# Five loads of x and four stores of a table, each issued as 120 and 8 partitions

## The chip, the core and the metric

The kernel runs on one core of a Trainium2 chip. Its time is the device time of one execution in microseconds; where several runs are named, the median of them. The core has five engines: TensorE (PE in the rows; PEld is its weight load), VectorE (DVE), ScalarE (ACT), GpSimd (POOL) and SyncE (SP). Transfers are issued from SP, ACT or POOL and carried out by 16 DMA engines that all queues share. SBUF, the on-chip memory, has 128 partitions.

## The reference

One layer of graph attention over N = 8192 nodes with F = 128 features, behind a layer norm. The adjacency matrix has some four ones in a row of 8192.

```python
h = jnp.maximum(_layernorm(x, axis=-1), 0.0)
# _L0_gnn_ref(h, adj, W, a):
h = x @ W
s_src, s_dst = h @ a[:F_out, 0], h @ a[F_out:, 0]
e = leaky_relu(s_src[:, None] + s_dst[None, :], negative_slope=0.2)
e = jnp.where(adj > 0, e, -9e15)
h_prime = softmax(e, axis=1) @ h
# result
x = x + h_prime
```

x is 8192 x 128 float32 (4 MB), adj is 8192 x 8192 int32 (256 MB), and the output has the shape of x.

## The kernel before

**Work.** The kernel never forms the dense attention. It reads all of adj once, finds in each row where the ones stand, and gathers only the rows of those neighbours from a table in DRAM. The table has one row of 130 numbers for each node: the 128 features of h @ W and the two scores of the node.

**First stage, the table.** SP issues five loads of x (L266, groups of 8, 8, 16, 16 and 16 tiles of 128 nodes). For each group VectorE computes the mean and variance of every row and from them 1/sqrt by Newton steps (`statistics`, L556 on); it waits for the load by the semaphore `x_loaded[k]`. ScalarE and GpSimd normalize (L431, L342), TensorE transposes (L1007), ScalarE takes the ReLU (L441), TensorE multiplies with W (L1017), ScalarE copies the rows of the table out of PSUM (L446). When a quarter of the rows is there, ScalarE issues its store to DRAM (`store_rows`, L458, four stores of 1040 KB: after steps 5, 9 and 13 of 16, and one at the end). GpSimd waits for the four semaphores `rows_stored[k]` before its first gather, since a gather may touch any row.

**Second stage, the batches.** adj comes in 32 batches of 256 rows. A batch is 8 units of 128 x 2048 numbers, and one load brings two units (L271, 2048 KB, 128 loads in all). `adj_buf` holds 8 units, so four loads are in flight or in use. SP issues the first four loads behind those of x, without a wait. Each later load waits until the two units of the batch before, whose place it takes, have been turned into masks (`mask_ready`). ScalarE makes the masks (L467, one instruction for a unit), apart from four of batch 0 that VectorE makes (L589). TensorE packs the masks into words (L1046, L1048), VectorE finds the set bits, GpSimd issues 14 gathers for each batch (L361), and VectorE forms the weighted sums into `x_all` (L820), from which SP stores the output at the end.

**Order.** Every engine runs its own list in program order, and semaphores tie them together. A transfer counts 16 on its semaphore when all of it has landed. A transfer issued from SP or ACT is queued behind the earlier ones of that issuer; the two issuers' queues are served side by side.

Of the kernel before, what the change touches and what calls it, by code (L numbers as in the profile page):

```python
# [4 lines left out]
P = 128  # L5
# [3 lines left out]
QUARTER = TILES // 4  # L9

STAT_GROUPS = [(0, 8), (8, 16), (16, 32), (32, 48), (48, 64)]
FOUR = 4
# [22 lines left out]
PART = N // PARTS  # L35
PART_BITS = BITS // PARTS
STORE_RUNS = ((0, 5), (5, 10), (10, 14), (14, 15))
SLOTS = 8
OWN = 6
SHARED = SLOTS - OWN  # L40
COLUMNS = 2 * OWN + SHARED
WIDE = 16
ROW = F + 2
S_COL, D_COL = F, F + 1
MORE = WIDE - SLOTS
REC = MORE + 4
# [36 lines left out]
def gat_kernel(nc, x, adj, W, a, out):  # L83
# [5 lines left out]
    mean_place, node_rows = table[0:1, :], table[1:1 + N, :]  # L89

    ctx = ExitStack()
    with ctx:
        def sb(name, shape, dt):
            return ctx.enter_context(nc.sbuf_tensor(name, shape, dt))

        def sem(name):
            return ctx.enter_context(nc.semaphore(name))
# [3 lines left out]
        mask_buf = sb("mask_buf", [P, UNITS, PART], bf16)  # L101
        gathered = sb("gathered", [P, BUFS, BATCH * SLOTS * ROW], f32)
        g_cols = [gathered[:, buf, :].rearrange("p (k n) -> p k n", n=ROW) for buf in range(BUFS)]

        g_view = [[g_cols[buf][:, b * OWN:b * OWN + SLOTS, :] for b in range(BATCH)] for buf in range(BUFS)]

        rows_all = gathered[:, :, :].rearrange("p a (t n) -> p (a t) n", n=ROW)

        x_all = sb("x_all", [P, TILES, F], f32)
# [43 lines left out]
        top = sb("top", [P, BATCH, WIDE], f32)  # L153
        skip = sb("skip", [P, BATCH, SLOTS], f32)
        index = sb("index", [P, BUFS, BATCH * SLOTS], u32)
        mine = sb("mine", [P, BATCH, SHARED], f32)
# [53 lines left out]
        x_loaded = [sem(f"x_loaded{k}") for k in range(len(STAT_GROUPS))]  # L210
# [5 lines left out]
        rows_stored = [sem(f"rows_stored{k}") for k in range(4)]  # L216
# [23 lines left out]
        def rows_of(dram, t, tiles):  # L240

            q, c = t // FOUR, t % FOUR
            return dram[q * FOUR * P:(q + 1) * FOUR * P, :].rearrange("(p c) n -> p c n", c=FOUR)[:, c:c + tiles, :]
# [5 lines left out]
        def group_of(i):  # L249

            return sum(1 for end in GROUP_ENDS if i > end)

        stores_in = [16 * (sum(1 for lo, _ in STORE_RUNS if group_of(lo * FOUR // BATCH) == g)
                           + (1 + BATCH if end == LAST else 0)) for g, end in enumerate(GROUP_ENDS)]
# [8 lines left out]
        @block.sync  # L263
        def _(sp):
            for k, (lo, hi) in enumerate(STAT_GROUPS):
                sp.dma_start(x_all[:, lo:hi, :].rearrange("p (q c) f -> p q (c f)", c=FOUR), x[lo * P:hi * P, :].rearrange("(q p c) f -> p q (c f)", p=P, c=FOUR)  # L266
                             ).then_inc(x_loaded[k], 16)

            def load_two(i, u):
                source = rows_of(adj, i * BATCH + u // PARTS, 1)[:, 0, u % PARTS * PART:(u % PARTS + 2) * PART]  # L270
                sp.dma_start(adj_buf[:, u:u + 2, :].rearrange("p u n -> p (u n)"), source).then_inc(adj_loaded[u // 2], 16)  # L271

            def load_batch(i):
                for u in range(0, UNITS, 2):

                    sp.wait_ge(mask_ready, (i - 1) * UNITS + u + 2)
                    load_two(i, u)

            def store_fours(lo, hi, group):

                sp.wait_ge(out_ready, hi * FOUR // BATCH)
                sp.dma_start(out[lo * FOUR * P:hi * FOUR * P, :].rearrange("(q p c) f -> p q (c f)", p=P, c=FOUR),
                             x_all[:, lo * FOUR:hi * FOUR, :].rearrange("p (q c) f -> p q (c f)", c=FOUR)
                             ).then_inc(out_stored[group], 16)

            def store_tiles(t, tiles, ready, group):
                sp.wait_ge(out_ready, ready)
                sp.dma_start(rows_of(out, t, tiles), x_all[:, t:t + tiles, :]).then_inc(out_stored[group], 16)

            for u in range(0, UNITS, 2):  # L290
                load_two(0, u)
            for i in range(1, BATCHES):
                load_batch(i)
            for lo, hi in STORE_RUNS:
                store_fours(lo, hi, group_of(lo * FOUR // BATCH))
            store_tiles((LAST - 1) * BATCH, BATCH, LAST, group_of(LAST))
            for b in range(BATCH):
                store_tiles(LAST * BATCH + b, 1, BATCHES + b, group_of(LAST))

            for g in range(GROUPS):  # L300
                sp.wait_ge(out_stored[g], stores_in[g])
            sp.wait_ge(w_stored, 16 * GROUPS)

            sp.wait_ge(verdict, 1)
            unfit_nodes = sp.value_load(unfit_n[0:1, 0:1], min_val=0, max_val=N)
            with sp.If(unfit_nodes > 0):

                sp.nop().then_inc(dn_out, 16)
                with sp.Fori(0, TILES) as t:

                    sp.wait_ge(dn_o, t + 1)
                    sp.dma_start(dense_adj, adj[bass.ts(t, P), :]).then_inc(dn_adj, 16)
                    sp.dma_start(x_row, x[bass.ts(t, P), :]).then_inc(dn_x, 16)
                    sp.dma_start(sd_row, node_rows[bass.ts(t, P), S_COL:ROW]).then_inc(dn_x, 16)
                    with sp.Fori(0, TILES // 4) as j:

                        sp.wait_ge(dn_mm, t * (TILES // 4) + j + 1)
                        sp.dma_start(h_blk, node_rows[bass.ts(j, 4 * P), 0:F].rearrange("(b p) f -> p b f", p=P)).then_inc(dn_h, 16)
                    sp.wait_ge(dn_o, t + 2)
                    sp.dma_start(out[bass.ts(t, P), :], o_row).then_inc(dn_out, 16)  # L320
                sp.wait_ge(dn_out, 16 * (TILES + 1))
# [3 lines left out]
        def _(pool):  # L325
# [26 lines left out]
            pool.wait_ge(mean_taken, 1)  # L352
            nc.gpsimd.dma_start(mean_place, mean_row[0:1, :]).then_inc(mean_stored, 16)
            for k in range(4):
                pool.wait_ge(rows_stored[k], 16)
            pool.wait_ge(mean_stored, 16)
            pool.wait_ge(sd_ready, 1)

# [54 lines left out]
        def _(act):  # L413
# [41 lines left out]

            def store_rows(k):
                act.wait_ge(rows_ready, (k + 1) * (FOURS // 4))
                act.dma_start(node_rows[k * QUARTER * P:(k + 1) * QUARTER * P, :].rearrange("(q p c) n -> p q (c n)", p=P, c=FOUR),  # L458
                              rows_all[:, k * QUARTER:(k + 1) * QUARTER, :].rearrange("p (q c) n -> p q (c n)", c=FOUR)
                              ).then_inc(rows_stored[k], 16)  # L460

            def mask(i, u):
                act.wait_ge(adj_loaded[u // 2], 16 * (i + 1))
# [64 lines left out]
        def _(dve):  # L528
# [24 lines left out]

            def statistics(k):
                lo, hi = STAT_GROUPS[k]
                dve.wait_ge(x_loaded[k], 16)  # L556
                settled()
                for t in range(lo, hi):
                    ins = v.bn_stats(stats[:, t - lo], x_all[:, t, :])  # L559
                done.add(ins)  # L560
                settled()
                for t in range(lo, hi):
                    ins = v.bn_aggr(mv_all[:, t, :], stats[:, t - lo])  # L563
                done.add(ins)
                settled()
                done.add(v.tensor_scalar(var_e[:, lo:hi], mv_all[:, lo:hi, 1], EPS, None, ALU.add))
                settled()

                square, factor = newton[:, 0, 0:hi - lo], newton[:, 1, 0:hi - lo]
                done.add(v.tensor_scalar(square.bitcast(i32), var_e[:, lo:hi].bitcast(i32), 1, None, ALU.arith_shift_right))  # L570
                settled()
                done.add(v.tensor_scalar(rstd[:, lo:hi].bitcast(i32), square.bitcast(i32), -1.0, float(MAGIC),
                                         ALU.mult, ALU.add))
                for _ in range(NEWTON_STEPS):
                    settled()
                    done.add(v.tensor_tensor(square, rstd[:, lo:hi], rstd[:, lo:hi], ALU.mult))  # L576
                    settled()
                    done.add(v.scalar_tensor_tensor(factor, square, -0.5, var_e[:, lo:hi], ALU.mult, ALU.mult))  # L578
                    settled()
                    done.add(v.scalar_tensor_tensor(rstd[:, lo:hi], factor, 1.5, rstd[:, lo:hi], ALU.add, ALU.mult))  # L580
                settled()
                v.scalar_tensor_tensor(nbias[:, lo:hi], mv_all[:, lo:hi, 0], -1.0, rstd[:, lo:hi], ALU.mult, ALU.mult  # L582
                                       ).then_inc(rstd_ready, (hi - lo) // FOUR)
# [588 lines left out]
```

## Time and profile before

| what | us |
|---|---|
| median of 3 runs (805.66 to 805.8) | 805.73 |
| the profiled execution: its own time | 804.8 |
| its span, from the first to the last instruction | 803.0 |
| busy: VectorE 606.7, ScalarE 526.8, TensorE 515.2, GpSimd 512.5 | |

The profiled execution is one run; what lies between its span and its own time (1.8 us) is outside the instructions. All starts in the rows below count from the start of the span. The busy times are sums over the whole span, so none of them alone says what bounds a stage.

### The profile page before, as it was taken

The numbers are of one execution on the slowest core, as the hardware profiler recorded it, in microseconds if no ns is written. First come the engines' busy times: TensorE is split into PE (matmuls) and PEld (weight loads), VectorE is DVE, ScalarE is ACT, GpSimd is POOL, SyncE is SP. The second block draws the span as 40 slices with busy tenths as digits, with TensorE's granted clock in tenths as the row PEclk, the third lists the DMA queues.
The fourth block names the chain that finished last, engine by engine and source line by source line (L and its number), as shares of the span: only waits on it lengthen the run. The fifth ranks groups of instructions, "written<-read, shape, count | busy, mean of one in ns | idle before, by whom it ended". The sixth has DMA issues, their size and how long they took to land.

```text
span 803.0 us, 9015 instructions
## 1 busy us (share of the span) xinstructions
PE 515.2 (64%) x1855; PEld 229.5 (29%) x1855; DVE 606.7 (76%) x3167; ACT 526.8 (66%) x371; POOL 512.5 (64%) x522
## 2 busy tenths in 40 slices
PE   3778666766577576666667676676767676656521
PEld 3652222322222232322222222222222232222221
DVE  7956678667776768777779778777786798888984
ACT  3879667676767767766767767676666767676300
POOL 4753776656666665577767666656777756775671
PEclk9888656676855766777666767667666556676655
DMA  8999999999999999999999999999999999999310
GB/s 334 423 386 390 406 403 406 409 411 407 408 408 409 409 407 401 406 398 393 380 406 397 405 396 399 392 408 397 400 389 398 389 399 399 389 380 402 120 37 15
DMA packets 40903, 299.31 MB, mean 373 GB/s; under 512 B 11052, under 2 KB 14034, under 8 KB 24464
## 3 DMA queue, kind: packets, MB, share of 16 engines
q1 hardware_dynamic: 22976, 276.83, 85.3%
q0 software_dynamic: 15328, 17.58, 6.9%
q10 hardware_dynamic: 2544, 4.33, 1.6%
q8 instruction: 15, 0.25, 0.1%
q14 instruction: 40, 0.33, 0.1%
HBM read 304.31 MB, written 8.65 MB: 390 GB/s over the span
## 4 chain that ended last, share of the span: by engine, by line
DMA 68%; DVE 10%; ACT 10%; issue 8%; PE 3%; POOLq 0%; ACTq 0%; DVEq 0%
DMA adj_buf<-in_adj 67%; ACT mask_buf L467 9%; DVE x_all L820 3%; PE banks L1048 2%; DVE stats L559 2%; PE banks L1017 1%; DVE mv_all L563 1%; DMA x_all<-in_x 1%; PE banks L1007 0%; DVE newton L576 0%; DVE rstd L580 0%; DVE newton L578 0%; PE banks L1089 0%; DVE mask_buf L589 0%; ACT work L431 0%
## 5 line engine op out<-in xcount | busy, mean ns | idle before, releaser
L467 ACT ACTIVATE mask_buf<-adj_buf,minus_half 128x2048 bf16<-128x2048 int32 x252 | 493.0, 1994 | 205.9 <-DMA adj_buf<-in_adj 205.4
L361 POOL DMA_INDIRECT gathered<-table,index x448 | 448.5, 1001 | 242.5 <-issue 145.9
L1048 PE MATMUL banks<-mask_buf,bit_ident 128*128 128x512 bf16 x1024 | 388.5, 527 | 99.8 <-ACT mask_buf L467 99.0
L1048 PEld LDWEIGHTS banks<-mask_buf,bit_ident 128*128 128x128 bf16 x1024 | 107.9, 124 | 325.7 <-ACT mask_buf L467 187.7
L820 DVE SCALAR_TENSOR_TENSOR x_all<-gathered,weight,x_all 128x128 f32<-128x128 f32 x512 | 157.7, 348 | 7.2
L635 DVE MAX8 words<-banks 128x8 f32<-128x512 f32 x64 | 44.7, 698 | 119.9 <-PE banks L1048 119.8
L1046 PE MATMUL banks<-key_rows,ones_b 3*128 3x512 bf16 x64 | 31.7, 495 | 119.2 <-ACT mask_buf L467 118.8
L1089 PE MATMUL banks<-x_all,one_hot 128*128 128x128 f32 x128 | 44.0, 445 | 18.3 <-DVE x_all L820 18.3
L1046 PEld LDWEIGHTS banks<-key_rows,ones_b 3*128 3x128 bf16 x64 | 6.1, 95 | 147.8 <-ACT mask_buf L467 145.9
L639 DVE MAX8 words<-rest 128x8 f32<-128x512 f32 x64 | 44.5, 695 | 2.2
L1089 PEld LDWEIGHTS banks<-x_all,one_hot 128*128 128x128 f32 x128 | 36.1, 317 | 27.5 <-DVE x_all L820 19.5
L637 DVE MATCH_REPLACE8 rest<-words,banks 128x512 f32<-128x512 f32 x64 | 43.5, 680 | 0.0
L342 POOL TENSOR_SCALAR work<-x_all,mv_all,rstd 128x128 f32<-128x128 f32 x32 | 30.9, 981 | 17.8 <-DVE nbias L582 15.9
L1090 PEld LDWEIGHTS banks<-max_sum,one_hot 128*128 128x128 f32 x128 | 33.6, 321 | 0.0
L387 POOL DMA_INDIRECT w_gathered<-table,w_index x24 | 24.0, 999 | 8.2 <-issue 6.7
L1090 PE MATMUL banks<-max_sum,one_hot 128*128 128x2 f32 x128 | 26.4, 276 | 0.0
L1074 PEld LDWEIGHTS banks<-rec,one_hot 128*128 128x128 f32 x128 | 22.7, 226 | 10.0 <-DVE one_hot L767 4.5
L784 DVE TENSOR_SCALAR e<-gathered,sd_all 128x8 f32<-128x8 f32 x64 | 13.3, 255 | 14.8 <-DMA gathered<-table,index 13.9
L1074 PE MATMUL banks<-rec,one_hot 128*128 128x12 f32 x128 | 19.8, 266 | 4.3 <-DVE one_hot L767 4.3
L1007 PE MATMUL banks<-ident,work 128*128 128x128 f32 x64 | 13.0, 338 | 14.1 <-ACT work L431 5.8
L1017 PE MATMUL banks<-w_ext,work 128*128 128x130 f32 x128 | 21.9, 326 | 0.0
L1017 PEld LDWEIGHTS banks<-w_ext,work 128*128 128x128 f32 x128 | 19.8, 235 | 1.2 <-ACT work L441 0.9
(162 smaller groups left out, 537.9 us busy)
## 6 DMA issues: line engine op xcount, KB each, us to landing
adj_buf<-in_adj SPq DMA_DIRECT2D x128, 2048.0 KB, 18.7
gathered<-table,index POOLq DMA_INDIRECT x448, 6.4
table<-gathered ACTq DMA_DIRECT2D x4, 1040.0 KB, 14.7
x_all<-in_x SPq DMA_DIRECT2D x3, 1024.0 KB, 10.8
out<-x_all SPq DMA_DIRECT2D x2, 1280.0 KB, 23.0
x_all<-in_x SPq DMA_DIRECT2D x2, 512.0 KB, 5.3
out<-x_all SPq DMA_DIRECT2D x1, 1024.0 KB, 25.5
w_gathered<-table,w_index POOLq DMA_INDIRECT x24, 5.3
```

Source lines behind the costliest of these rows:

```text
L361: nc.gpsimd.indirect_dma_start(g_cols[buf][:, k, :], None, table, bass.IndirectOffsetOnAxis(index[:, buf, k:k + 1], 0), bounds_check=N, oo ...
L467: nc.scalar.activation(mask_buf[:, u], adj_buf[:, u], ACT.Sign, bias=minus_half[:]).then_inc(mask_ready, 1)
L635: done.add(v.max(words[:, b, 0:8], bank))
L637: v.match_replace(rest[:, b], words[:, b, 0:8], bank, -float(1 << BITS)).then_inc(words_read, 1)
L639: done.add(v.max(words[:, b, 8:16], rest[:, b]))
L820: ins = v.scalar_tensor_tensor(at[b], g_view[par][b][:, k, 0:F], weight[:, b, k:k + 1], at[b], ALU.mult, ALU.add)
L1017: ins = mm(banks[:, 2 + 2 * par + b // 2, at:at + ROW], relu_t[par][:, b], w_ext[:], start=True, stop=True)
L1046: mm(bank, ones_b[0:3, :], key_rows[0:3, :], start=True, stop=False)
L1048: ins = mm(bank, bit_ident[:, h * PART_BITS + c], mask_buf[:, u, c * BIT_COLS:(c + 1) * BIT_COLS], start=False, stop=(h == PARTS - 1 and c ...
L1074: ins = mm(banks[:, 3, 0:REC], one_hot[:, i % BUFS, b], rec[:, i % BUFS, b], start=False, stop=False)
L1089: mm(banks[:, bank, 0:F], one_hot[:, i % BUFS, b], x_all[:, i * BATCH + b, :], start=False, stop=False)
L1090: ins = mm(banks[:, bank, F:SUMS], one_hot[:, i % BUFS, b], max_sum[:, i % BUFS, b], start=False, stop=False)
```

## The change

Each of the five loads of x and each of the four stores of the table is issued as two transfers: one for partitions 0 to 119 (`LIGHT = 120`) and, right behind it on the same queue, one for partitions 120 to 127. Both count 16 on the same semaphore, and those who wait for it now wait for 32. The bytes, their places in DRAM and SBUF and all else stay as they were. The loads of adj and the stores of the output are not touched.

```diff
+LIGHT = 120
...
             for k, (lo, hi) in enumerate(STAT_GROUPS):
-                sp.dma_start(x_all[:, lo:hi, :].rearrange("p (q c) f -> p q (c f)", c=FOUR), x[lo * P:hi * P, :].rearrange("(q p c) f -> p q (c f)", p=P, c=FOUR)
-                             ).then_inc(x_loaded[k], 16)
+                place = x_all[:, lo:hi, :].rearrange("p (q c) f -> p q (c f)", c=FOUR)
+                rows = x[lo * P:hi * P, :].rearrange("(q p c) f -> p q (c f)", p=P, c=FOUR)
+                sp.dma_start(place[0:LIGHT], rows[0:LIGHT]).then_inc(x_loaded[k], 16)
+                sp.dma_start(place[LIGHT:], rows[LIGHT:]).then_inc(x_loaded[k], 16)
...
             for k in range(4):
-                pool.wait_ge(rows_stored[k], 16)
+                pool.wait_ge(rows_stored[k], 32)
...
-                act.dma_start(node_rows[k * QUARTER * P:(k + 1) * QUARTER * P, :].rearrange("(q p c) n -> p q (c n)", p=P, c=FOUR),
-                              rows_all[:, k * QUARTER:(k + 1) * QUARTER, :].rearrange("p (q c) n -> p q (c n)", c=FOUR)
-                              ).then_inc(rows_stored[k], 16)
+                place = node_rows[k * QUARTER * P:(k + 1) * QUARTER * P, :].rearrange("(q p c) n -> p q (c n)", p=P, c=FOUR)
+                rows = rows_all[:, k * QUARTER:(k + 1) * QUARTER, :].rearrange("p (q c) n -> p q (c n)", c=FOUR)
+                act.dma_start(place[0:LIGHT], rows[0:LIGHT]).then_inc(rows_stored[k], 16)
+                act.dma_start(place[LIGHT:], rows[LIGHT:]).then_inc(rows_stored[k], 16)
...
-                dve.wait_ge(x_loaded[k], 16)
+                dve.wait_ge(x_loaded[k], 32)
```

SP's list at the start of the program, before; a row is a line, an operation, what it writes and reads, its shape, and how often it stands in a row:

```order
1 L266 DMA x_all<-in_x 128x2x512 x2
2 L266 DMA x_all<-in_x 128x4x512 x3
3 L271 DMA adj_buf<-in_adj 128x4096 x4
4 L271 DMA adj_buf<-in_adj 128x4096 [waits mask_ready] x124
5 L282 DMA out<-x_all 128x5x512 [waits out_ready] x2
```

The same place in the changed kernel:

```order
1 L269 DMA x_all<-in_x 120x2x512
2 L270 DMA x_all<-in_x 8x2x512
3 L269 DMA x_all<-in_x 120x2x512
4 L270 DMA x_all<-in_x 8x2x512
5 L269 DMA x_all<-in_x 120x4x512
6 L270 DMA x_all<-in_x 8x4x512
7 L269 DMA x_all<-in_x 120x4x512
8 L270 DMA x_all<-in_x 8x4x512
9 L269 DMA x_all<-in_x 120x4x512
10 L270 DMA x_all<-in_x 8x4x512
11 L274 DMA adj_buf<-in_adj 128x4096 x4
12 L274 DMA adj_buf<-in_adj 128x4096 [waits mask_ready] x124
```

Ten transfers now stand ahead of the first load of adj, in place of five.

ScalarE's list where the first stage ends, before (the last two copies of table rows, the fourth store, the masks of units 6 and 7 of batch 0, and the first masks of batch 1):

```order
73 L446 COPY gathered<-banks 128x520 [waits projected] x2
74 L458 DMA table<-gathered 128x4x520 [waits rows_ready]
75 L467 ACTIVATE mask_buf<-adj_buf,minus_half 128x2048 [waits adj_loaded3,mask_ready]
76 L467 ACTIVATE mask_buf<-adj_buf,minus_half 128x2048 [waits adj_loaded3]
77 L467 ACTIVATE mask_buf<-adj_buf,minus_half 128x2048 [waits part_packed,adj_loaded0] x2
```

The same place in the changed kernel:

```order
76 L449 COPY gathered<-banks 128x520 [waits projected] x2
77 L463 DMA table<-gathered 120x4x520 [waits rows_ready]
78 L464 DMA table<-gathered 8x4x520
79 L471 ACTIVATE mask_buf<-adj_buf,minus_half 128x2048 [waits adj_loaded3,mask_ready]
80 L471 ACTIVATE mask_buf<-adj_buf,minus_half 128x2048 [waits adj_loaded3]
81 L471 ACTIVATE mask_buf<-adj_buf,minus_half 128x2048 [waits part_packed,adj_loaded0] x2
```

One more issue stands between the last copy and the first mask of this stretch; the three earlier stores have gained one each in the same way.

## Rows read from the trace of the kernel before

**Rows 1.** The page: span and DMA issues (KB each, median us to landing)
```profile
span 803.0 us, 9015 instructions
...
adj_buf<-in_adj SPq DMA_DIRECT2D x128, 2048.0 KB, 18.7
gathered<-table,index POOLq DMA_INDIRECT x448, 6.4
table<-gathered ACTq DMA_DIRECT2D x4, 1040.0 KB, 14.7
```

**Rows 2.** Busy time by stretch, all engines (last three: PE clock, DMA share, GB/s)
```profile
2.00:17.00 15.00, 4.91 (x19) 3.95 (x19) 11.50 (x71) 5.61 (x14) 5.38 (x8) 1.00 0.97 357
17.00:60.00 43.00, 32.73 (x196) 26.75 (x196) 32.51 (x161) 33.98 (x74) 27.33 (x29) 0.84 1.01 407
60.00:80.00 20.00, 15.99 (x61) 5.84 (x61) 12.65 (x62) 19.65 (x12) 6.92 (x7) 0.83 0.99 389
80.00:740.00 660.00, 441.97 (x1505) 180.72 (x1502) 502.31 (x2626) 458.01 (x265) 438.38 (x439) 0.68 1.00 400
```

**Rows 3.** Waits: in total us, times, longest; ACT
```profile
ACT mask_buf L467 <- DMA adj_buf<-in_adj: 205.4, 119, 3.0
```

**Rows 4.** Waits of the DMA queue of SyncE
```profile
SPq L271 <- ACT mask_buf L467: 664.3, 122, 21.5
```

**Rows 5.** Line 271 (loads of adj) from 100 to 700 us
```profile
L271 SPq DMA_DIRECT2D adj_buf<-in_adj x106: 327/328/328, 101.6 to 695.3; - x106
...
DMA to landing us min/median/max: 17.5/18.7/19.7
```

**Rows 6.** Chain that ended last, 0 to 10 us (start, us, what)
```profile
0.75 4.26 DMA x_all<-in_x
...
5.04 1.66 DVE stats L559 x8
```

**Rows 7.** The same chain, 60 to 80 us
```profile
62.10 0.86 ACT mask_buf L467
...
63.99 5.14 ACT mask_buf L467 x3
...
75.46 16.38 DMA adj_buf<-in_adj
```

**Rows 8.** Line 266 (loads of x), whole execution
```profile
L266 SPq DMA_DIRECT2D x_all<-in_x x5: 449/474/699, 0.8 to 3.0; - x5
...
DMA to landing us min/median/max: 4.3/8.6/13.7
```

**Rows 9.** ScalarE in order of time, 50 to 58 us
```profile
55.30 0.59 ACT L446 COPY gathered<-banks 128x520 f32<-128x520 f32 x1 [0.48 <-PE banks L1017]
55.92 0.38 ACTq L458 DMA_DIRECT2D table<-gathered  x1
56.40 2.00 ACT L467 ACTIVATE mask_buf<-adj_buf,minus_half 128x2048 bf16<-128x2048 int32 x1 [0.51 <-ACT gathered L446]
```

**Rows 10.** ScalarE in order of time, 56 to 90 us
```profile
56.40 22.82 ACT L467 ACTIVATE mask_buf<-adj_buf,minus_half 128x2048 bf16<-128x2048 int32 x12 [0.51 <-ACT gathered L446]
79.57 3.90 ACT L467 ACTIVATE mask_buf<-adj_buf,minus_half 128x2048 bf16<-128x2048 int32 x2 [0.35 <-DMA adj_buf<-in_adj]
86.21 3.89 ACT L467 ACTIVATE mask_buf<-adj_buf,minus_half 128x2048 bf16<-128x2048 int32 x2 [2.74 <-DMA adj_buf<-in_adj]
```

**Rows 11.** Line 458, the fourth store alone
```profile
L458 ACTq DMA_DIRECT2D table<-gathered x1: 378/378/378, 55.9 to 55.9; - x1
...
DMA to landing us min/median/max: 8.3/8.3/8.3
```

**Rows 12.** Line 271, the eighth load of adj alone
```profile
L271 SPq DMA_DIRECT2D adj_buf<-in_adj x1: 327/327/327, 60.3 to 60.3; - x1
```

**Rows 13.** GpSimd in order of time: the first gather
```profile
71.25 1.08 POOL L361 DMA_INDIRECT gathered<-table,index  x1 [14.27 <-issue]
```

**Rows 14.** DMA issues of a short store near the end
```profile
out<-x_all SPq DMA_DIRECT2D x1, 256.0 KB, 2.3
```

## The prediction

> **What bounds the kernel now.** I began with the page and the busy time by stretch. The adjacency loads are 128 of 2048 KB [rows 1], 268 MB against some 17 MB for x, table and output. From 80 to 740 us the DMA engines are busy all the time (share 1.00, 400 GB/s) while the busiest computing engine, VectorE, works 502 of 660 us [rows 2]. The waits say the same: ScalarE waited 119 times, 205.4 us in all, for a load of adj before a mask [rows 3], and SP waited 664.3 us for masks before it could issue the next load [rows 4]. So there is a loop: load, mask, next load into the same place. From the first to the last of 106 loads pass 593.7 us, so 593.7 / 105 = 5.65 us for each; a load lands 18.7 us after its issue [rows 5], which is 3.3 loads. Something always stands in the queue, the transfers run back to back, and the end is set by how soon the DMA engines are through with all of adj. After the last load comes a tail of computation that simply moves with it.
>
> The first stage is different. Its chain goes through the first load of x (4.26 us), then VectorE's statistics [rows 6], then ScalarE and TensorE. From 56.40 to 79.2 ScalarE makes twelve masks without a pause; the next mask waits 0.35 us for its load, the one after 2.74 us [rows 10]. So at 79 us ScalarE and the DMA engines are level, and from there the DMA engines lead.
>
> **The change, part by part.** It removes no byte. It adds nine issues, and it may change how the bytes fall on the 16 engines. I number three terms.
>
> *Term 1, five more issues on SP.* One issue of a load of x takes 0.449 to 0.699 us, median 0.474 [rows 8]. Only the first group is urgent: VectorE starts at 5.04, right when the load has landed at 0.75 + 4.26 = 5.01 [rows 6]. The second piece is issued 0.45 to 0.5 us behind the first, and the wait is now for both. If all of that shows, the first stage starts 0.5 us later; if the small piece lands beside the large one, 0. I take 0.4, near the issue's own time, since the small piece can't be requested before. The later four loads have cover: their issues end at 3.6 us now and at some 6 us then, and VectorE is still at work on earlier groups. The first loads of adj go out 5 x 0.5 = 2.5 us later, but they stand behind x in the queue: the last load of x, issued at 3.0, needs 13.7 us [rows 8], up to 16.7. What covers them is that backlog; without it they would cost 2.5 us.
>
> *Term 2, four more issues on ACT.* One takes 0.378 us [rows 11]. The first three lie in a stretch in which ScalarE's issue runs beside its computing, and I give them nothing (all three on the path would be 1.1 us). The fourth does not: the last copy runs until 55.89, the store is issued at 55.92 for 0.38, and the first mask starts at 56.40 after 0.51 us of idle time [rows 9]. Behind that mask wait all the others, the eighth load of adj, which SP issues at 60.3 when units 6 and 7 are masked [rows 12], and the masks at 62.1 to 75 that are on the chain [rows 7]. So +0.38, taken as 0.4. GpSimd now waits for all eight pieces of the table. The last store landed at 55.9 + 8.3 = 64.2 [rows 11] and the first gather started at 71.25 [rows 13], so 7 us of cover lie there, and a store later by 1 or 2 us costs nothing.
>
> *Term 3, which engines carry the bytes.* 128 partitions over 16 engines are 8 each, and 120 are 8 each for 15. If the large piece goes to 15 engines, one engine is left without any of x and of the table, and the 8 small rows fall on others. No row shows the engines apart. What rows say is that all transfers of 128 partitions give each engine the same, so the load of adj as a whole lands when the slowest engine is through. If the spared engine is that one, it has a head start into the stream. How large? Not the whole of what it is spared: before 60.3 us SP holds back the loads, and an engine without work just idles. The head start counts from the eighth load on, issued at 60.3 [rows 12]. A lone store of 256 KB lands 2.3 us after its issue [rows 14], of which 0.6 us is moving it at 407 GB/s [rows 2]; the rest, 1.7 us, is what passes before and after the data. So the eighth load could begin to flow at 60.3 + 1.7 = 62.0, while the fourth store is not through until 64.2. The spared engine gains up to 2.2 us. Upper bound: the whole of one store's share, 1040 KB (1.065 MB) / 407 GB/s = 2.6 us. Lower bound: 0, if the spared engine is not the last. I take 2.2. From then on this engine has always something queued (3.3 loads), so the head start is kept up to the last load. The sum for the likeliest case is 0.4 + 0.4 - 2.2 = -1.4 us. That both delays count in full in that case is because the spared engine now waits for the issue of the eighth load, which they move.
>
> The Trainium skill's page "DMA: Bandwidth & Descriptors", section "Why a DMA increments its semaphore by 16 and not by 1", says that a transfer uses the largest number of engines up to 16 that divides its outer dimension, the lowest-numbered ones; and its section "Latency and other measured facts" calls engines 7 and 15 usually the slower ones. By these two the large piece spares engine 15 and the small one goes to engines 0 to 7. No row here shows it. Against the change speaks the same page's section "Rules for kernel authors": two transfers to disjoint partition halves share the same engines, so use one. By that alone the sum would be terms 1 and 2, +0.8 us.
>
> The sum is made against the profiled execution (span 803.0 us [rows 1], its own time 804.8, 0.9 us below the median 805.73): span 801.6. On the median: 805.73 - 1.4 = 804.3.
>
> **The rivals.**
>
> *A, the spared engine is the slowest one:* 804.3, as above; by its bounds (terms 1 and 2 together 0 to 1.9, term 3 between 0 and 2.6) from 803.1 to 807.6, most of it from 803.2 to 805.5. Chance 0.45. For it speaks that the share of the engines is 1.00 and yet the rate falls from 407 to 400 GB/s [rows 2], as it would if one engine lagged behind; but the gathers' small transfers explain that as well.
>
> *B, the slowest engine gets the small pieces.* The end is later. Its price: x is 4.19 MB and the table 4.26 MB, together 8.45 MB / 407 GB/s = 20.8 us of moving for an even spread; an engine that carries nine rows in place of eight needs 1/8 more, 2.6 us. It counts in full if that engine has never been idle since 2 us, and rows 2 give shares of 0.97, 1.01 and 0.99 up to 80 us. Terms 1 and 2 fall away here, since the backlog covers them. 805.73 + 2.6 = 808.3. It decides from the point at which the slowest engine is among those that carry the extra rows; nothing later heals it, as that engine stays the last. Were it not the last, ScalarE would see 0.5 to 2.5 us more of waiting at 79 us and nothing at the end. Chance 0.14. By the Trainium skill's page named above, this is the case in which engine 7 and not engine 15 is the slowest.
>
> *C, nothing binds.* The slowest engine is among those with 8 rows as before, or the bytes are spread over 16 engines in another way. Terms 1 and 2 shift only work that the backlog covers: 805.7, up to 806.5 if the shift reaches the stream. Chance 0.24. Waits at 79 and 86 us would hardly change.
>
> *D, a larger head start.* The spared engine is the last one already before 60 us, and the third store's share (2.6 us) lies ahead of its eighth load too. 804.3 - 2.6 = 801.7. Against it: the fourth store was through 3.9 us after the eighth load was issued, little more than one store's share and the latency. Chance 0.13.
>
> *E, the small pieces are slow in themselves.* Ten more issues delay VectorE's first group by the length of a whole first load, 4.26 us [rows 6], instead of 0.4. The first stage moves by that, so does ScalarE's run of masks, which is level with the DMA engines at 79 us: 805.73 + 3.9 - 2.2 = 807.4 with the head start. Chance 0.04.
>
> **How the numbers follow.** What a measurement of this kernel can tell from no change is about 0.2%, 1.6 us. Case A gives faster beyond that (below 804.1) in a good four tenths of its chance, 0.20, else no difference, 0.25; D gives faster, 0.13; C gives the same, 0.22, and slower 0.02; B slower, 0.12, and same 0.02; E slower or same, 0.02 and 0.02. Sums: faster 0.33, same 0.51, slower 0.16. The range leaves out the lower half of D (0.06) and the upper half of B with the tail of E (0.08): 801.8 to 808.2.
>
> **What the profile of the changed kernel would show.** Term 1: VectorE's first statistics at 5.4 instead of 5.04. Term 2: two issues of about 0.38 us behind the last copy, the first mask at 57.2 instead of 56.40, and the eighth load at 61.1 instead of 60.3. Term 3: the loads from the eighth to about the twelfth land no sooner, since 15 engines have the same work as before, but ScalarE waits less in the stretch behind, and the last issue of adj is some 1.4 us earlier; the time for a load from 100 us on is unchanged at 5.65 us when taken late in the stream. Wrong would be: a last load later than before (B), or one shifted by exactly the first stage's delay (then the backlog covers nothing). The prediction falls if the stream's own pace changes, since nothing that I count touches it.

## The result and the profile after

The changed kernel takes 816.04 us (median of 4 runs, 815.29 to 817.54), the kernel before in the same session 805.69 us (4 runs, 805.33 to 805.8): 10.35 us more, a ratio of 1.0132 (95% interval 1.0114 to 1.0149). Forecast were 804.3 us, in a range from 801.8 to 808.2. It is slower, and by four times what the dearest of the rivals gave.

The page of the changed kernel: its span and the DMA queues (packets, MB, share of the 16 engines).

```profile
span 814.4 us, 8992 instructions
...
q1 hardware_dynamic: 23011, 276.83, 85.4%
```

The span is 11.4 us longer than in [rows 1]; the queue's bytes and its share are the same as before to a tenth. So no byte was added, and the longer span holds as much more time in packets. The busy time by stretch says where (last two columns: DMA share, GB/s):

```profile
2.00:17.00 15.00, 4.82 (x19) 3.95 (x19) 10.75 (x67) 4.86 (x12) 4.63 (x7) 1.00 0.98 209
17.00:60.00 43.00, 26.88 (x162) 23.69 (x163) 31.33 (x160) 29.30 (x71) 28.07 (x28) 0.76 1.02 376
60.00:80.00 20.00, 15.47 (x77) 6.84 (x77) 12.62 (x62) 16.43 (x13) 1.02 (x2) 1.00 0.97 361
80.00:740.00 660.00, 438.59 (x1467) 177.83 (x1495) 493.64 (x2577) 459.61 (x265) 441.67 (x442) 0.66 1.01 401
```

In [rows 2] the first stretch moved 357 GB/s, here it moves 209 at the same share of 0.98: the engines are as busy and carry little more than half. Missing are 148 GB/s over 15 us, 2.22 MB; 31 GB/s over the 43 us to 60, 1.33 MB (the last loads of x fall into it); and 28 over the 20 us to 80, 0.56 MB. That is 4.11 MB, 10.3 us at the 400 GB/s of the stream: the whole loss, and over half of it is made before 17 us. From 80 us on nothing has changed, 401 GB/s against 400. The loads of adj from 100 to 700 us (line 274 is line 271 of before):

```profile
L274 SPq DMA_DIRECT2D adj_buf<-in_adj x107: 327/328/328, 100.6 to 699.2; - x107
...
DMA to landing us min/median/max: 17.5/18.7/19.6
```

(699.2 - 100.6) / 106 = 5.65 us for a load, landing after 18.7, as in [rows 5]. The stream has its old pace and starts later. The chain that ended last, in the first 40 us:

```profile
4.86 2.88 SPq L270
7.78 23.30 DMA adj_buf<-in_adj
31.53 1.48 issue
```

Before, the chain went through VectorE's statistics [rows 6]; now it goes through the first load of adj, which stands behind x in the queue and lands at 7.78 + 23.30 = 31.1 us. In the first stage VectorE waited once for x before, 1.5 us; now that wait is 2.3 us, and a new one of 5.6 us for adj has joined it. The waits of VectorE from 0 to 60 us (total, times, longest):

```profile
DVE mask_buf L593 <- DMA adj_buf<-in_adj: 5.6, 1, 5.6
DVE stats L563 <- DMA x_all<-in_x: 2.3, 1, 2.3
```

And ScalarE in order of time where the first stage ends:

```profile
61.96 0.59 ACT L449 COPY gathered<-banks 128x520 f32<-128x520 f32 x1 [0.47 <-PE banks L1021]
62.58 0.34 ACTq L463 DMA_DIRECT2D table<-gathered  x1
62.95 2.41 ACTq L464 DMA_DIRECT2D table<-gathered  x1
65.46 2.00 ACT L471 ACTIVATE mask_buf<-adj_buf,minus_half 128x2048 bf16<-128x2048 int32 x1 [2.91 <-issue]
```

The last copy starts 6.66 us later than in [rows 9], and the second of the two issues takes 2.41 us, where one took 0.38; the first mask of this stretch starts at 65.46 instead of 56.40.

The profile has no row for when a load of x in two pieces has landed as a whole. The trace records each engine's own increment of the semaphore, and the last of them is the landing. Worked out from these records, landing of the five loads in us from the start of each kernel's span, for all kernels of this study that touch x or the stores; the row of the changed kernel is the second (the expectations quoted below name some of them up to 0.1 us off):

```
before          5.0    7.5   10.4   13.1   16.8
after           5.8    8.7   14.5   20.6   26.4
x_only          5.9    8.9   14.7   21.0   26.9
x_columns       5.6    7.2   10.2   12.9   15.6
x_64_64         6.0    8.4   13.2   18.0   23.3
x_112_16        5.2    8.6   13.0   17.7   22.3
x_last          5.0    7.5   10.2   13.7   20.0
stores_only     5.0    7.5   10.4   13.1   16.2
```

The fifth load lands 9.7 us later than before, which is nearly the whole loss of 10.35. The same records show 25 increments for each of the changed loads: one at the issue and 15 landings for the piece of 120 partitions, one at the issue and 8 for the piece of 8. So the large piece does run on 15 engines, as term 3 supposed. What it supposed beside that, that each of the 15 takes as long as before, is false.

### The profile page after: what moved, and what is told of

Same layout as the page of the kernel before. It is cut to its first block, busy times and chain, and to the rows that moved or that the text cites. A ratio compares the mean times of both kernels' runs of the same rounds, so it can differ in the third digit from the quotient of the medians.

```text
span 814.4 us, 8992 instructions
## 1 busy us (share of the span) xinstructions
PE 512.3 (63%) x1823; PEld 228.4 (28%) x1855; DVE 604.7 (74%) x3167; ACT 526.9 (65%) x371; POOL 513.4 (63%) x522
## 4 chain that ended last, share of the span: by engine, by line
DMA 71%; ACT 11%; issue 9%; DVE 6%; PE 2%; SPq 1%; ACTq 0%; POOLq 0%; DVEq 0%
DMA adj_buf<-in_adj 71%; ACT mask_buf L471 8%; DVE x_all L824 2%; ACT work L434 1%; PE banks L1052 1%; ACT prob L485 1%; PE banks L1021 1%; SPq L270 1%; ACT gathered L449 0%; PE banks L1011 0%; ACT work L444 0%; SPq L269 0%; DVE rest L641 0%; PE banks L1093 0%; DVE words L643 0%
## 5 line engine op out<-in xcount | busy, mean ns | idle before, releaser
L1093 PE MATMUL banks<-x_all,one_hot 128*128 128x128 f32 x128 | 41.8, 426 | 18.8 <-DVE x_all L824 18.8
L1093 PEld LDWEIGHTS banks<-x_all,one_hot 128*128 128x128 f32 x128 | 33.8, 298 | 26.6 <-DVE x_all L824 19.9
L1094 PEld LDWEIGHTS banks<-max_sum,one_hot 128*128 128x128 f32 x128 | 31.9, 306 | 0.0
## 6 DMA issues: line engine op xcount, KB each, us to landing
adj_buf<-in_adj SPq DMA_DIRECT2D x128, 2048.0 KB, 18.7
```

The lines of the kernel that those rows point to most:

```text
L1093: mm(banks[:, bank, 0:F], one_hot[:, i % BUFS, b], x_all[:, i * BATCH + b, :], start=False, stop=False)
L1094: ins = mm(banks[:, bank, F:SUMS], one_hot[:, i % BUFS, b], max_sum[:, i % BUFS, b], start=False, stop=False)
```

## The experiments

### Which half of the change costs

Of the kernel before, only the loads or only the stores were cut:

```diff
 # x_only
+                sp.dma_start(place[0:120], rows[0:120]).then_inc(x_loaded[k], 16)
+                sp.dma_start(place[120:128], rows[120:128]).then_inc(x_loaded[k], 16)
```

> Only the five loads of x are issued as 120 and 8 partitions; the stores stay whole. Theory P (the loads themselves run slowly: in the changed kernel the fifth load of x had landed at 26.5 us in place of 16.8, and all transfers behind it are that much later): the loss is nearly all here, 9 to 10 us over before, 815 us. Rival Q (the stores: ScalarE's last issue took 2.41 us, and GpSimd's first gather waited for the pieces): under 1 us over before, 806 us. Rival R (the number of issues as such): 5 of 9 issues, about half of the loss, 811 us.

Measured: 815.76 us against 805.22 (ratio 1.0126, 1.0101 to 1.0152), 10.5 us over.

```diff
 # stores_only: each store as [0:120] and [120:128]
-                pool.wait_ge(rows_stored[k], 16)
+                pool.wait_ge(rows_stored[k], 32)
```

> Only the four stores of the table are issued as 120 and 8 partitions; the loads of x stay whole. Theory P: no loss, 805 to 806 us; if the engine that is spared by a piece of 120 partitions is the slowest of the 16, a gain of up to 2.2 us less 0.4, so 804 us. Rival Q: nearly all of the loss, 812 us or more. Rival R: 4 of 9 issues, 810 us. The last issue on ScalarE takes 0.3 to 0.4 us by P, since the queue isn't late, and 2.4 us by Q.

Measured: 806.08 us (1.0017, 1.0002 to 1.0031), 0.9 us over. So the loads of x carry the whole loss (theory P), and rival Q falls: the stores do not cost it. Rival R, the number of issues as such, does not fit either (it had 811 and 810 us). ScalarE in the kernel with the cut stores:

```profile
55.84 0.59 ACT L446 COPY gathered<-banks 128x520 f32<-128x520 f32 x1 [0.47 <-PE banks L1020]
56.46 0.34 ACTq L458 DMA_DIRECT2D table<-gathered  x1
56.83 1.20 ACTq L461 DMA_DIRECT2D table<-gathered  x1
58.13 2.00 ACT L470 ACTIVATE mask_buf<-adj_buf,minus_half 128x2048 bf16<-128x2048 int32 x1 [1.70 <-issue]
```

Even with the loads of x whole, the last issue took 1.20 us where P expected 0.3 to 0.4, and the first mask started 1.73 us later than in [rows 9]. No head start appeared. The store packets themselves are not slower: their median (2080 B each) is 89 ns in the kernel before and 89 ns with the cut stores.

### Is it the number of pieces?

```diff
 # x_columns: 128 partitions in both pieces, half of each partition's bytes
+                half = (hi - lo) // FOUR // 2
+                sp.dma_start(place[:, 0:half], rows[:, 0:half]).then_inc(x_loaded[k], 16)
+                sp.dma_start(place[:, half:], rows[:, half:]).then_inc(x_loaded[k], 16)
```

> The five loads of x are issued as two pieces each, both over 128 partitions, each with half of the bytes of a partition; as many issues as in the changed kernel. Theory P (what costs is how the partitions are cut): the fifth load lands at 17 to 17.5 us, time 805.7 to 806.3 us. Rival R (the number of issues): 811 us or more, as in the run with x alone.

Measured: 805.77 us (1.0003, 0.9987 to 1.0019), no difference, with ten issues as in the change. The fifth load landed at 15.6 us, sooner even than before. Ten transfers in place of five cost nothing; what costs is where the partitions are cut.

### Fifteen engines, or ports?

```diff
 # x_64_64
+                sp.dma_start(place[0:64], rows[0:64]).then_inc(x_loaded[k], 16)
+                sp.dma_start(place[64:128], rows[64:128]).then_inc(x_loaded[k], 16)
```

> The five loads of x are issued as two pieces of 64 partitions. Two forms of theory P: by P1 (the pieces collide at the side of SBUF: at any time the engines write to partitions that reach only half of the ports), the loads of x take twice as long here too, the fifth lands at 26 to 27 us, and the time is 815 us. By P2 (a transfer on 15 engines, or an uneven one, is slow), 64 partitions are 4 for each of 16 engines, nothing is slow, and the time is 806 us.

Measured: 812.64 us (1.0086, 1.0062 to 1.011), 7.4 us over, the fifth load at 23.3 us. All 16 engines take part here (32 landings for each load), and it is slow. P2 is refuted, for it had 806. P1 had the direction, but 815 and 26 to 27 us were too much. The busy time from 6 to 12 us, when SP's queue moves nothing but x, shows it best: first with whole columns, then with 64 and 64 partitions.

```profile
6.00:12.00 6.00, 0.56 (x2) 0.50 (x2) 5.45 (x36) 1.45 (x5) 1.22 (x2) 1.00 1.02 385
```

```profile
6.00:12.00 6.00, 0.56 (x2) 0.50 (x2) 5.45 (x35) 1.13 (x4) 0.90 (x2) 1.00 1.07 220
```

385 against 220 GB/s at full share: 0.57. The changed kernel has 216 in the same stretch:

```profile
6.00:12.00 6.00, 0.56 (x2) 0.50 (x2) 5.45 (x36) 1.32 (x4) 1.09 (x2) 1.00 1.03 216
```

```diff
 # x_112_16
+                sp.dma_start(place[0:112], rows[0:112]).then_inc(x_loaded[k], 16)
+                sp.dma_start(place[112:128], rows[112:128]).then_inc(x_loaded[k], 16)
```

> The five loads of x are issued as 112 and 16 partitions, so each piece can be spread over all 16 engines, 7 and 1 partitions for each. The fifth load lands between the two known cases (16.8 us whole, 26.8 us with 120), at 20 to 23 us, and the time is 808 to 812 us. Theory P2 (only a transfer on fewer than 16 engines is slow): 806 us.

Measured: 810.25 us (1.006, 1.0037 to 1.0083), 5.1 us over, the fifth load at 22.3 us, 238 GB/s from 6 to 12 us: inside what P1 gave, and P2 fails again.

Both runs leave open on which side of a transfer the engines get into each other's way, reading DRAM or writing SBUF. So x was copied from DRAM to DRAM, with the same reads, ahead of everything else:

```diff
 # dram_copies
+            for a, cuts in enumerate((((0, P),), ((0, 64), (64, P)))):
+                for k, (lo, hi) in enumerate(STAT_GROUPS):
+                    place = copy[a, lo * P:hi * P, :].rearrange("(q p c) f -> p q (c f)", p=P, c=FOUR)
+                    rows = x[lo * P:hi * P, :].rearrange("(q p c) f -> p q (c f)", p=P, c=FOUR)
+                    for at, end in cuts:
+                        sp.dma_start(place[at:end], rows[at:end]).then_inc(copied, 16)
```

> The kernel before with copies of x from DRAM to DRAM ahead of its loads, once in five whole pieces of 128 rows of 2 KB, once in ten pieces of 64, with the same reads as the loads of the run with 64 and 64. It tells on which side the slowness lies. Theory P1 (ports of SBUF): without SBUF the two forms run alike, their packets of 2 KB take the same time and the two copies take equal time. Rival D (the order in which DRAM is read): the second form is half as fast, as it is into SBUF. The end of the kernel moves by the time of the copies, 20 to 60 us; that number tells nothing.

One run, 831.84 us; its total says nothing here, since the copies are extra work. The busy time while the whole copies ran (4 to 12 us) and while those of 64 and 64 ran (16 to 24 us):

```profile
4.00:12.00 8.00, 0.59 (x3) 0.50 (x2) 0.00 (x0) 0.42 (x2) 0.00 (x0) 1.00 0.98 321
16.00:24.00 8.00, 0.00 (x0) 0.00 (x0) 0.00 (x0) 0.00 (x0) 0.00 (x0) 1.00 1.05 332
```

321 and 332 GB/s: with the same reads and no SBUF, cutting at 64 costs nothing. The packets say the same. From the trace's packet records, the median duration of a packet of 2 KB is 84 ns in both copies; in the loads of x, taken over each 2 us from 6 to 12 us, it is 84 to 85 ns before, 147 to 160 ns in the changed kernel and 155 to 165 ns with 64 and 64. The slowness sits on the way into SBUF, and rival D is refuted for the cut at 64; the cut at 120 was not copied in this way.

So the ports are an argument and not a finding: shown is that the loss lies on the way into SBUF and goes with how the partitions are cut, and no run shows which engine writes which partition.

### Does lost DMA time in the first 20 us reach the end?

```diff
 # x_last: only the fifth load (k == 4) in two pieces
+                for a, b in ((0, 120), (120, P)) if k == 4 else ((0, P),):
+                    sp.dma_start(place[a:b], rows[a:b]).then_inc(x_loaded[k], 16)
```

> Only the fifth load of x, a quarter of its bytes, is cut into 120 and 8 partitions. It lands some 2.5 us later, at 19 us, and VectorE needs it only at 33.7 us. Theory S (the lost time of the DMA engines is the loss, since they are never idle up to the end): a quarter of the loss of all five, 2.5 us, so 808 us. Rival T (the loss comes by the statistics that start late): nothing, 805 to 806 us.

Measured: 809.65 us (1.0059, 1.004 to 1.0079), 4.5 us over; the fifth load landed at 20.0 us, 3.2 later. ScalarE, from the last store on:

```profile
55.95 0.38 ACTq L460 DMA_DIRECT2D table<-gathered  x1
56.43 15.25 ACT L469 ACTIVATE mask_buf<-adj_buf,minus_half 128x2048 bf16<-128x2048 int32 x8 [0.51 <-ACT gathered L448]
72.19 3.90 ACT L469 ACTIVATE mask_buf<-adj_buf,minus_half 128x2048 bf16<-128x2048 int32 x2 [0.51 <-DMA adj_buf<-in_adj]
```

Its masks begin at 56.43, as in [rows 9], so the first stage is on time; but after 8 masks it waits for a load, where before it made 12 without one [rows 10]. Theory S holds and T falls: DMA time lost before 20 us is lost at the end, and computation that is on time doesn't help. The size is above S's 2.5: the load was 3.2 us late, and 1.3 us more are not accounted for. They may be scatter: the interval of the ratio reaches down to 3.2 us, and the profiled execution, the fastest of the six, took 807.98 us, 2.8 over.

Over the runs, lateness of the fifth load and loss of time go together: 10.1 and 10.5 us (x_only), 9.7 and 10.35 (the change), 6.5 and 7.4 (64 and 64), 5.5 and 5.1 (112 and 16), 3.2 and 4.5 (the fifth alone). With columns the fifth load landed 1.2 us sooner, and the time did not change.

### Is the spared engine the slowest?

Each of these adds a store of a constant tile to DRAM in batches 4 to 31, which the kernel doesn't need, with 16 KB for each engine that takes part:

```diff
 # extra_128, extra_120, extra_88: n = 128, 120, 88
+                if i >= EXTRA_FROM:
+                    sp.dma_start(scratch[i, 0:n, :], bit_ident[0:n, 0:8, :].rearrange("p c n -> p (c n)")).then_inc(extra_stored, 16)
 # extra_8, extra_7: n = 8, 7, eight times with 2 KB a partition
+                    for j in range(8):
+                        sp.dma_start(scratch[i, n * j:n * j + n, :], bit_ident[0:n, 0:8, :].rearrange("p c n -> p (c n)")).then_inc(extra_stored, 16)
```

> The kernel before, with one more store in each of the batches 4 to 31: 128 partitions of 2 KB each of a constant tile, issued by SP behind the batch's loads of adj, to a place of its own in DRAM. It adds work that the reference has not; the output is untouched. It is the scale for the next run: 28 stores of 256 KB on all 16 engines at 400 GB/s are 18 us, so 823 us, as the stream is bound by the DMA engines.

> The same 28 extra stores, of 120 partitions: by the landings of the changed kernel such a piece leaves one of the 16 engines without bytes and gives the others the same as before. Theory A (the spared engine is the slowest, and alone sets the stream's pace): little is added, 806 to 812 us. Theory C (the slowest engine is another): as much as with 128 partitions, some 823 us. The part of term 3 of the prediction that gave a head start holds by A and falls by C.

Measured: 822.5 us with 128 partitions (1.0216, 1.0188 to 1.0243) and 822.1 us with 120 (1.0209, 1.018 to 1.0238), against 805.18. Both cost 17 us, as theory C expected.

> The extra stores again, of 88 partitions: 8 partitions for each of 11 engines, and none for five. With 120 partitions they cost as much as with 128, so the slowest engine is not the one that 120 spares. If it is among the 11: some 17 us over before again, 822 us. If it is among the four engines that this run spares in addition: little is added, 806 to 812 us.

> In place of each extra store eight stores of 8 partitions, each of 2 KB a partition: the same 16 KB on each of the eight engines that the small pieces of the change use, nothing on the others. Case B of the prediction (the slowest engine is one that gets the small pieces): 17 us over before, 822 us. Case C (it is another): little, 805 to 810 us, apart from the eight issues.

> As with 8 partitions, but each extra store has 7, so the engines that carry it are one fewer: the eighth is spared. With 8 partitions the run took 32 us over before, and one engine's landings came 11 to 14 us behind those of seven others, so the slowest engine is one of the eight. If it is the eighth: its landings are not among those of the extra stores, and little is added, 805 to 812 us. If it is one of the first seven: 836 us again.

Measured: 826.35 us with 88 partitions, 836.89 with 8, 838.72 with 7 (1.027, 1.039, 1.0422; before 804.76, 804.76 and 805.06). That is 21.6, 32.1 and 33.7 us over, where the expectations for the first two had 17 us for the same 16 KB on each engine. A packet of 2 KB took 84 ns (median) in all five kernels, so the rest of it is not in the packets; where it comes from stays open. Since all of them cost much, the time alone would leave room for another reading, that the engines used become slow by the extra work. The semaphore records decide it. Landings of the extra stores from 600 us on, grouped where 1.5 us pass without one:

```
extra_128   611.5 to 613.9 us: 15     623.8 us: 1
            635.7 to 637.5 us: 15     647.3 us: 1
extra_120   613.3 to 615.3 us: 14     625.1 us: 1     629.5 us: 1
extra_88    615.3 to 617.3 us: 10     627.5 us: 1     631.6 us: 1
extra_8     602.1 to 606.2 us: 56     613.5 to 614.8 us: 8     618.1 to 620.5 us: 8
extra_7     601.0 to 604.4 us: 48     612.1 to 613.4 us: 8     616.5 to 618.9 us: 8
```

With 128 partitions 15 engines land within 2.4 us and one comes some 10 us behind. In every other kernel two groups follow the large one: one is the increment at the next issue (for each store one), the other the late engine. 14 + 1, 10 + 1, 7 x 8 + 8 and 6 x 8 + 8: the late one is among the 15, the 11, the 8 and the 7 engines. The kernel before, without any extra store, has the late engine too, in its loads of adj: one issued at 598.6 us has 15 increments from 605.9 to 608.8 us and the last at 616.9. It falls behind by and by: at 74 us all 16 increments of such a load still lie within 1.4 us, and at 98 us one comes 1.9 us behind the other 15.

So one engine runs some 8 to 12 us behind all others late in the stream, whether there is extra work or not. It is not the one that 120 partitions spare, and in the last run it is among the seven that 7 partitions use. If a transfer on fewer engines always takes the first ones of the same order, it is then not the eighth either. The traces don't name the engines, and these runs were made on three chips (128 and 120 on one, 88 and 8 on another, 7 on a third), so it is assumed and not shown that the late engine is the same in all of them.

## Why the prediction was wrong

**What bounds the kernel** was read rightly: the stream's pace did not move (5.65 us a load, 400 and 401 GB/s), and the run with the fifth load alone shows that DMA time is the bound even before 20 us. That should have been turned into a question for each transfer that changes shape: does it still run at its old rate?

**Term 3 is the step that failed:** "128 partitions over 16 engines are 8 each, and 120 are 8 each for 15", and with it the sentence that 15 engines have the same work as before. They have the same bytes, but the rate was taken from whole transfers (407 GB/s) for pieces that had no row. The loads ran at 216 GB/s from 6 to 12 us, where the kernel before has 373 and the one with columns 385, and the fifth landed 9.7 us late. No term and no rival priced that; the range was built from bounds on latency and on bytes, none on the rate. The runs with 64 and 64 and with the copies in DRAM put the cause on the way into SBUF.

**The head start** of 2.2 us, the other half of term 3, didn't exist. The extra stores speak against cases A and D: with 120 partitions the late engine is among the 15 used, so the spared one is not it. In the changed kernel one engine was through with its part of the first load of adj at 20.7 us and the other 15 from 29.5 to 31.1: one engine was some 10 us ahead, as it would be if spared, and the load as a whole waited for the others. Case B, at a chance of 0.14, had the right engine (the late one is among those that carry pieces of 8 partitions) and, at 2.6 us, the wrong price for what happened, so its direction came out by luck; whether its 1/8 more bytes cost anything by themselves can't be seen beneath the 10 us, and the cut stores alone show at most 0.9 us.

**Term 1** gave 0.4 us. VectorE started at 5.79 instead of 5.04, 0.75 later, and with columns at 5.65, 0.61 later; yet with columns the ten issues cost nothing in the end. So the delay is real, somewhat larger than taken, and not on the path. Rival E, with VectorE's first group 4.26 us late, is not what happened: the small pieces delay little, and the large ones are slow.

**Term 2** was mis-sized: the extra issue behind the last copy took 2.41 us in the changed kernel and 1.20 with the stores alone, not 0.38. With the stores alone the first mask came 1.73 us later (58.13 instead of 56.40), and the kernel lost 0.9 us. In the kernel with x alone the store took 0.38 and the loss was as large as in the changed one, so this stall isn't what costs. Nor does waiting behind unlanded stores alone explain it, since in both kernels none of the three earlier stores had landed by then (the first landed at 64.5 and 63.2 us).

**The cover of 7 us** for GpSimd was used up: the last store of the table landed at 82.6 us instead of 64.3, and the first gather started at 84.1 instead of 71.25. That is not what costs either: with x alone the first gather started at 92.5 and the loss was the same.

**The cover of 2.5 us** for the later issue of the first adj loads was real: with columns the first of them was issued 2.8 us later (6.42 instead of 3.60) and nothing was lost. But the cover for VectorE's later work was gone: the backlog grew by 10 us, and the first stage came to wait for loads of adj (5.6 us on VectorE).

**The signs.** All loads of adj, before and in the changed kernel (shortest, median and longest issue in ns, first and last start in us):

```profile
L271 SPq DMA_DIRECT2D adj_buf<-in_adj x128: 327/328/3212, 3.6 to 729.3; - x128
L274 SPq DMA_DIRECT2D adj_buf<-in_adj x128: 327/328/1209, 7.8 to 738.7; - x128
```

The last load was issued 9.4 us later, where the prediction had 1.4 us earlier, and a later last load was its own sign of being wrong. Two slips in its numbers change nothing: x, the table and the output are 12.6 MB together and not some 17, and rival E's "ten more issues" on SP are five.

## What to carry to other kernels

Where the DMA engines are the bound, a load that covers fewer or other partitions than 0 to 127 has to be priced by rate and not by bytes; 128 partitions cut along the free axis cost nothing here, 112, 120 and 64 cost between 36 and 44% of the rate (238, 216 and 220 GB/s where whole loads had 373 to 385). A transfer early in the kernel is on the path as soon as the queue behind it never runs empty, even if those who wait for it have time. And before an engine is spared, show that it is the slow one: the semaphore's increments tell how many of a transfer's engines are late, and transfers on fewer engines tell whether the late one is among those.

## What the runs showed that I had not expected

- A piece of 120 partitions runs on 15 engines and one of 88 on 11, by the number of landings (15 and 11); into SBUF the 15 move 216 GB/s where 16 move 373 to 385, out of SBUF no such loss shows (a packet of the table's store takes 89 ns whole and cut at 120, the kernel with the cut stores takes 806.08 us, and 28 extra stores cost 17 us with 120 and with 128 partitions).
- One of the 16 engines runs behind the rest, in the kernel before as well: late in the stream its landing comes 8 to 10 us behind those of the 15 others. Why, no run here shows.
- The issue of a transfer can itself stall: SP's tenth piece of x took 2.88 us where its neighbours took 0.3 to 0.6, and ScalarE's last issue 2.41 us. It is not a matter of cut partitions: in the kernel before, SP's sixth issue, the first load of adj, took 3.21 us. With columns none of the fourteen first issues of SP took over 1 us. What decides it was not measured.
